# Two-layer recurrent kernel: the last expert tile steps of the layer-2 rows stand one place sooner

## What is computed

```
xn = layernorm(x)
x  = x + attention(xn) * silu(ffn(xn))
```

## Time and profile before

| | before |
|---|---|
| median of 3 runs | 2049.53 us (2042.01 to 2052.2) |
| profiled execution, its own time | 2047.19 us |
| its span, first to last instruction | 2045.2 us |
| granted TensorE clock, mean over the span | 0.961 |
| busy: PE, PEld, DVE, ACT, POOL | 1741.8, 1255.9, 1280.8, 996.9, 220.7 us |
| HBM read, written | 96.45 MB, 61.69 MB |

### The profile page before, as it was taken

The page is one execution under the profiler, slowest core; times in us unless marked ns, Lnnn a source line. Parts: engine busy times, 40 slices in busy tenths (PEclk is TensorE's granted clock), DMA queues, the critical chain, the costliest instruction groups (busy, mean ns, idle before and its releaser), DMA issues.

```text
span 2045.2 us, 60865 instructions
## 1 busy us (share of the span) xinstructions
PE 1741.8 (85%) x23060; PEld 1255.9 (61%) x23060; DVE 1280.8 (63%) x3518; ACT 996.9 (49%) x2242; POOL 220.7 (11%) x235
## 2 busy tenths in 40 slices
PE   5999999998999999958888888886889899889562
PEld 3665666556666666735666666765666676666562
DVE  5677777775766666656666766766666666665311
ACT  2444444444555555534655456553555454555242
POOL 0000000000000000020111011101111110110122
PEclk9899999998999999989999999998999999999887
DMA  4222222222222112221221222110122211111473
GB/s 141 86 95 95 95 95 95 95 95 81 62 74 73 44 53 74 96 95 45 73 68 56 68 70 77 55 37 24 62 64 65 65 60 46 49 56 39 159 245 112
DMA packets 97579, 160.62 MB, mean 79 GB/s; under 512 B 14729, under 2 KB 66057, under 8 KB 94090
## 3 DMA queue, kind: packets, MB, share of 16 engines
q1 hardware_dynamic: 88170, 135.05, 20.1%
q0 software_dynamic: 9248, 23.17, 3.7%
HBM read 96.45 MB, written 61.69 MB: 77 GB/s over the span
## 4 chain that ended last, share of the span: by engine, by line
PE 53%; DVE 16%; issue 11%; ACT 9%; SPq 5%; DMA 3%; POOL 2%; DVEq 0%; ACTq 0%; POOLq 0%
PE psum L920 5%; PE psum L799 4%; PE psum L777 3%; PE psum L1224 3%; PE psum L910 3%; PE psum L1115 3%; PE psum L1074 2%; PE psum L808 2%; PE psum L959 2%; PE psum L844 2%; PE psum L1012 2%; PE psum L848 2%; PE psum L1140 2%; PE psum L1005 2%; PE psum L1044 2%
## 5 line engine op out<-in xcount | busy, mean ns | idle before, releaser
L1455 ACT ACTIVATE pts<-psum 128x512 f32<-128x512 f32 x192 | 99.1, 603 | 170.6 <-PE psum L959 170.0
L684 POOL DMA_INDIRECT rows<-h,recA x64 | 64.3, 1004 | 828.8 <-DVE recA L1680 699.6
L1942 DVE TENSOR_REDUCE mneg<-psum 128x2 f32<-128x512 f32 (+1 forms) x192 | 119.1, 684 | 54.7 <-PE psum L939 35.2
L920 PE MATMUL psum<-wa,xT_s 128*128 128x512 f32 x256 | 122.7, 625 | 0.0
L799 PE MATMUL psum<-txT,wt 128*128 128x128 f32 x864 | 116.7, 278 | 5.7 <-DVE st L1949 3.0
L708 POOL DMA_INDIRECT rows<-xn,recC x32 | 34.7, 1083 | 751.2 <-DVE recC L2122 647.3
L1074 PE MATMUL psum<-xT_s,wa 128*128 128x256 f32 x512 | 115.7, 380 | 0.0
L799 PEld LDWEIGHTS psum<-txT,wt 128*128 128x128 f32 x864 | 107.9, 195 | 8.9 <-DVE st L1949 4.0
L1074 PEld LDWEIGHTS psum<-xT_s,wa 128*128 128x128 f32 x512 | 96.3, 191 | 13.0 <-issue 0.8
L808 PE MATMUL psum<-wt,tg 128*128 128x128 f32 x528 | 78.4, 279 | 16.5 <-DVE tg L1647 16.5
L1645 DVE TENSOR_TENSOR tg<-tg,psum 128x256 f32<-128x256 f32 x84 | 35.2, 419 | 78.0 <-ACT tg L1319 77.1
(11 more groups left out here) (276 smaller groups left out, 4292.1 us busy)
## 6 DMA issues: line engine op xcount, KB each, us to landing
wt<-in_wB SPq DMA_DIRECT2D x84, 384.0 KB, 2.9
outs<-pbd SPq DMA_DIRECT2D x16, 1024.0 KB, 7.0
wt<-in_wD SPq DMA_DIRECT2D x24, 578.0 KB, 3.5
wa<-in_wD SPq DMA_DIRECT2D x15, 578.0 KB, 3.6
tx<-rows SPq DMA_DIRECT2D x132, 64.0 KB, 2.9
outs<-ty SPq DMA_DIRECT2D x132, 64.0 KB, 1.6
rows<-pbd SPq DMA_DIRECT2D x64, 128.0 KB, 1.8
rows<-pbd SPq DMA_DIRECT2D x8, 1024.0 KB, 3.9
```

Source lines behind the costliest of these rows:

```text
L920: mm(bank(f"{name}{t}{c}"), xnT[:, t * P:(t + 1) * P], wqkv0[:, off + c * 512:off + (c + 1) * 512], start=True, stop=True).then_inc(*fills ...
L1455: af(pT[:, n, :], bank(f"e{n}"), ACT.Exp, scale=float(HD) ** -0.5).then_inc(*frees(f"e{n}"))
L1942: ins = v.tensor_reduce(mneg[:, int(n >= 4), col:col + hs], sc, AX.X, ALU.max, negate=True)
```

## The change

Steps 4, 5 and 6 stand one place sooner in all four orders (the uses of PSUM, PE, ACT, DVE); step 7 keeps its place and now follows w2 directly. Step 4 stands behind the chunk-state products (on ACT behind the copies of o, on DVE behind `slots` and the tile table), step 5 takes the place that 4 had, and step 6 stands between the feed-forward products, ahead of w2. Nothing is added or removed, and SP's and POOL's programs are the same. In D rows only step 4 has work, its one ty.

```diff
--- before.py
+++ after.py
@@ -130,16 +130,16 @@
         names += [f"st{n}" for n in range(NC - 1)]
         tile_step(3)
         names += [f"o{ch}{hh}" for hh in range(2) for ch in range(2)]
+        tile_step(4)
         first_z()
         names += ["wo1"]
-        tile_step(4)
+        tile_step(5)
         first_qk("lq")
         names += ["z2T"]
         names += ["f0", "f1"]
         first_qk("lk")
-        tile_step(5)
+        tile_step(6)
         names += ["w2"]
-        tile_step(6)
         tile_step(7)
     else:
         over("wo", "hT", "gate", "oT00", "oT01", "oT10", "oT11", "s0")
```

## The result

| | before | after |
|---|---|---|
| median | 2050.86 us (4 runs, 2042.01 to 2053.02) | **2024.78 us** (4 runs, 2023.21 to 2030.06) |
| profiled execution, its own time | 2047.19 us | 2026.13 us |
| its span | 2045.2 us | 2024.1 us |
| granted clock, mean over the span | 0.961 | 0.964 |

The ratio of after to before is **0.9882, 95% interval 0.9859 to 0.9905**: 24.2 us faster. Forecast were 2030.0 us, a range of 2021 to 2041 and faster.

A forecast was written before the change was run, and what follows sets the result against it. TensorE's order was taken to set the row pace, and transfers the last stage, F. Rows with B tiles -14.3, D rows -1.2, last D row and F -3.0 sum to -18.5 us: 2030 us, range 2021 to 2041.

The forecast's parts named there:

- End of the row: Key products to next row, rows with B tiles: 4.11 us instead of 7.12, 3.0 us sooner.
- Middle of the row: Step 4 before the next input's transposes fills 0.64 us of waits a row; z products come 0.8 us later.
- those before L777 of aden and L844 fall under 1: Sign of being right: TensorE's waits before the next input's transposes (1.7 us) and z products (2.8 us) fall under 1.
- Clean rows: Rows with B tiles: 2.2 us less per row, 3.0 less 0.8, counted for six rows as 13.2.
- The seventh row: Last row with B tiles: half the gain, 1.1 us, since the last tiles' stores follow, with the record ahead of them.
- D rows: Only ty2 moves; 0.17 us of wait filled a row, -1.2 us over seven rows, ends 0 and -2.5.
- The last D row and F: Last stage F's first load comes 3.5 us sooner; 3.0 us counted as gain, ends 0 and 3.6.
- some 2 us: Most that the last feed-forward would give back, once, if TensorE's clock fell to 1.2 GHz after ty2 left.
- Rival 1: Waits move rather than go: 0.9 us a row, 6.3 over seven, F nothing, about 2043 us; chance 0.15.
- Rival 2: Slower by the clock: falls at the z products and wo1 cost +36 us against -18.5, 2067 us; chance 0.05.
- Rival 3: Falls of the clock in rows with B tiles go with the waits: 5 us more, 2025 us; chance 0.10.
- Rival 4: VectorE's order paces the row, so removed TensorE waits return; only the F term is left, 2047 us; chance 0.06.

The follow-up runs named there:

- step 6 alone: In rows with B tiles only step 6 moved, ahead of w2, against the kernel before: 2043.42 us, ratio 0.9965.
- VectorE's step 5 later: Changed kernel with VectorE alone taking its step 5 behind the evacuation of z2T: 2033.16 us, ratio 0.9909 to the kernel before.
- the first two groups: First two of three groups of follow-up runs, five rounds each; the unchanged kernel's median was 2051.51 us in the first, 2054.38 in the second.
- the two repeats: The unaltered change measured again in two later groups against the kernel before: 2030.31 and 2052.85 us, ratio 0.9899 each.
- the third group of runs: Last group of follow-up runs, five rounds: the change a third time and two variants; the unchanged kernel's median was 2071.33 us.

## Why the prediction was right, and where not

*End of the row:* right. 2.87 us a row (7.12 to 4.25) where 3.0 was forecast, by the same chain: th5 reached ScalarE 1.10 behind its start and ty5 came 3.47 behind it. That it takes the moves together was not in the prediction; it treated step 6 as the part that brings the gain and the others as its cost.

*Middle of the row:* right in size, wrong in its sign to look for. From the chunk-state products to the z products the fourth row is 0.8 us longer (5.49 to 6.28), as forecast. But "those before L777 of aden and L844 fall under 1" holds for the first alone (1.7 to 0.0); L844's went from 2.8 to 3.5. Both stand behind the same hand-over: the transposes came later, VectorE's two evacuations followed at once, and TensorE waits for the second as long as ever, only from a later start. A wait that is filled ahead of a chain of two engines moves the chain, and the wait inside it stays.

*Clean rows:* the fourth, sixth and seventh B rows are 1.96, 2.15 and 2.18 us shorter, forecast 2.2. The idle time of the seven, -13.9, is the forecast's -14.3.

*The seventh row:* forecast half, 1.1 us. It gained 2.18 and the next row gave back 1.9. The prediction said that the record "now stands ahead of" the stores "with less room between", which is the cause, and it should have priced it: it took half where nearly all was lost.

*D rows:* forecast -1.2 for seven, that is 0.17 a row. The four rows that can be compared are 0.3 shorter each; the sum of the seven is lost in their scatter, in the first profile in one fall of the clock (a row of 61.49 us at 0.97 where it was 59.44). The end of the second of them, after:

```profile
1606.21 1.95 PE L1248 MATMUL psum<-wa,pts 128*128 128x128 f32 x16
1606.72 2.48 DVE L1792 COPY reg<-psum 128x512 f32<-128x512 f32 x4 [0.51 <-ACT big L1384]
...
1609.44 0.42 DVE L2145 TENSOR_TENSOR recC<-xn,psum 128x256 f32<-128x256 f32 x1 [0.24 <-DVE reg L1792]
...
1609.92 0.39 PE L1084 MATMUL psum<-dmask,identb 128*128 128x512 bf16 x1 [1.75 <-DVE recC L2145]
```

The next row's L1084 waits 1.75 us for the last residual (L2145), which stands right behind VectorE's key copies (L1792), and these behind ScalarE; from w2 to that residual are 3.23 us, where it was 3.04 (1629.02 to 1632.06 in the profile before). So "I take it that the end of the row follows the query products" holds, by way of ScalarE and VectorE and not of TensorE, and the ends named for it, 0 and -2.5, hold what was found.

*The last D row and F,* after, as the earlier trace rows, with TensorE's first tile of F:

```profile
1886.68 0.17 DVE L1719 CAST tab<-st 1x42 int32<-1x42 f32 x1
1886.78 0.27 DVE L1655 TENSOR_TENSOR ty<-psum,wt 128x128 f32<-128x128 f32 x1
...
1889.67 0.35 SPq L567 DMA_DIRECT2D wa<-in_wD  x1
...
1895.65 2.05 PE L1248 MATMUL psum<-wa,pts 128*128 128x128 f32 x16 [0.93 <-ACT pts L1524]
...
1897.53 0.38 PE L777 MATMUL psum<-ident,tx 128*128 128x128 f32 x2
```

The load comes 42.94 us after the row's start, where it came at 46.93: 4.0 us sooner in this pair. Over the seven profiles with the move it comes at 42.9 to 45.0, over the three without at 45.9 to 47.0, 2.5 us sooner on average, forecast 3.5. VectorE's copy follows the tile table at once, as worked out. The forecast kept 3.0 because "TensorE's own end of the last row may become the next thing" for F's first tile. It did: that tile (L777) now follows w2 with no wait for its load, at 50.80 to 54.60 us of the row, where it was at 49.93 to 50.98. The stretch is 1.9 shorter even so.

The last feed-forward did fall to 1.2 GHz (granted 0.50 from 1891.73 to 1894.23), as the prediction worked out against this place. TensorE waits ahead of z2T (L777 of xr) and then runs f0 and f1, before:

```profile
1911.08 0.44 PE L777 MATMUL psum<-ident,xr 128*128 128x128 f32 x2 [1.97 <-DVE xr L1614]
1912.16 2.00 PE L1238 MATMUL psum<-xT_s,wa 128*128 128x256 f32 x8 [0.64 <-DVE xT_s L2135]
```

and after:

```profile
1890.03 0.44 PE L777 MATMUL psum<-ident,xr 128*128 128x128 f32 x2 [3.97 <-DVE xr L1614]
1891.10 3.61 PE L1239 MATMUL psum<-xT_s,wa 128*128 128x256 f32 x8 [0.64 <-DVE xT_s L2136]
```

The wait grew by 2.0 us, where the prediction had 0.9. In all ten profiles that have ty2 moved it is 3.1 to 4.0 us and f0 and f1 take 3.50 to 3.78; in the three that have not it is 1.97 and they take 2.00. In five of the ten w2 too takes 3.65 to 3.79 instead of 2.05. The prediction named "some 2 us" for this at most and had it in its sum at nothing; it is 1.5 to 3.5 us of TensorE's time. How much of it reached the end is not shown: F's own transfers set its pace, and among the seven the stretch does not follow the first tile (177.49 us with that tile at 54.00, 177.95 with it at 51.38).

*The rivals.* Rival 1 had the waits move rather than go; they did so in part with step 6 alone and with VectorE's step 5 later, not in the change itself. Rival 2, slower by the clock, went the other way in the B rows. Rival 3, that the falls of the clock go with the waits, 5 us, with a chance of 0.10, came true beside the forecast: 6.1 us in the B rows by the slices, in a busy time that fell by 7.6. The CP row took 1.9 back, and F kept 1.1 less than forecast. With idle time -13.9, busy time -7.6, CP row +1.9, D rows -1 (the four that can be compared) and F -1.9 the parts come to -22.5 us, between the -24.2 of the first measurement and the -20.7 (0.9899 of 2050.86 is 2030.1) of the two repeats. That the forecast of 2030 is so near the repeats is partly luck: the sum had the clock of the B rows and that of the last feed-forward at nothing, and only half of the loss behind the seventh row, and these partly cancel. Over the 118 runs of the first two groups, compared within each kernel and group, the time falls by 1.0 us for each 0.001 of mean granted clock, and the means are 0.957 to 0.958 for kernels with the old B rows and 0.960 to 0.962 for the changed ones: some 3 us. Rival 4, VectorE paces, holds for the D rows' end and the stretch from f0 to th5, not for the wait removed.

## What to carry to other kernels

Where steps of a software pipeline (transposes, first product, second product of tiles) are threaded through other work by hand, look at the distance between neighbouring steps, in the time that the other engines need to hand one back (here 3.3 to 3.5 us): two steps side by side expose what their own work leaves of that time (0.9 and 1.8 us here), and moving one of them alone moves the wait to the next pair. Count a wait of TensorE of nearly 2 us or more ahead of dense work twice, since its clock may fall behind it: it did at 13 of 24 row ends behind 1.83 us, at none of three places behind 1.97, and at ten of ten behind 3.1 to 4.0. Look for such a wait where the moved work came from, here the last D row. And if stores come sooner by such a change, see what else stands in their queue ahead of them before counting the row's gain.

## What the runs showed of the hardware that was not expected

A store of the last tile took 1.53 us from issue to landing with the 2.48 us older record ahead of it on SP's queue, or with the record behind it, and 3.43 to 3.74 us with a record 1.17 us older. The record itself, four times as large, lands 2.9 to 3.1 us after its issue (257 KB against 64), so the younger store starts while the record is still under way. The Trainium skill, "DMA: Bandwidth & Descriptors", "Queues, rings and completion order", says that descriptors of a ring are taken in their order; the two landing times agree with it. Whether the order or shared bandwidth holds the store up is not shown.

TensorE's clock fell at a row's start to a granted 0.66 to 0.73 over 5 us in which TensorE was busy for all of them, behind a wait of 1.83 us at 13 of 24 row ends, and did not with waits of 1.42 and less at any of 54. The wait alone does not decide it: behind the 1.97 us ahead of the last row's z2T, in the three profiles that have it, f0 and f1 took 2.00 us, and behind 3.1 to 4.0 us at the same place 3.50 to 3.78, in ten of ten. And in the third group of runs everything was 1% slower (before 2071.33 against 2051.51 and 2054.38 us), on the chip of the second group, with the ratio of the change the same to four digits, 0.9899.
